# Feed forward by seven block products, hidden units through DRAM, and the third layer norm moved into the attention turns

## Chip, cores and metric

One core of one Trainium2 chip. The metric is the device time of one execution in microseconds (us), the median of repeated runs. PE is the matrix engine, PEld its weight load, DVE the vector engine, ACT the scalar engine, POOL is GpSimd, SP is the queue that issues all DMAs.

## What is computed

One decoder layer on x, 16 sequences of 128 rows by 1024 columns, all in fp32:

```
x = x + attn(layernorm(x))              # qkv 1024 -> 3072, clip, layer norm of q and k, 32 heads, Wout
x = x + xattn(layernorm(x), ctx)        # 8 heads of 64, linear attention, column norm
h = layernorm(x)
a = h @ W1.T ; b = h @ W3.T             # 1024 -> 2752, weights as 4-bit words times a scale per group of 64
x = x + (silu(a) * b) @ W2.T            # 2752 -> 1024
```

## The kernel before

**Arithmetic.** A big product is made in three passes: an operand is split into a high part (ACT copies it into the engine's reduced fp32 type) and a low part (DVE subtracts the high part from it), and PE sums high by high, high by low and low by high. Each matmul here is 128 x 128 weights by 512 columns.

**Phases.** `qkv_phase` writes q, k and v to DRAM. `attention_phase` runs 17 turns, `turns(eng, turn)`: turn b does the self attention of sequence b (`own`), the cross attention of sequence b-1 (`cross`), and prepares sequence b+1 (`ahead`). A turn has 12 steps t, written out in one fixed order for each engine (`turn_tensor`, `turn_scalar`, `turn_vector`, `turn_gpsimd`, `turn_sync`), and ends with the projections. In a step, PE forms scores (L527), turns the normalised scores (L519), forms queries of the cross attention (L537), keys (L558, even steps) and turns the keys (L564, odd steps) in the PSUM pair `pair_k`, which ACT empties (L669 into kT). DVE adds the bias to the scores (L481), takes maxima and sums. The last operation of a sequence is `res<-v_in,res` on POOL (L728, semaphore `fin`), after which SP stores `res` to x2 in DRAM.

**Feed forward.** `feed_forward_phase` handles the 16 sequences in two halves of 8. A half first loads x2 into `acc` (L1003, L1007, L1018), normalises it (`LayerNormT`: statistics on DVE L63 to L69, `normalise` on POOL L76 and L79, eight transposes on PE L86, high part on ACT L92, low part on DVE L96). Then it loops over 22 tiles of 128 hidden units, two to a group. For a tile, DVE unpacks the words (L1077 shifts, L1087 times scale), ACT takes the high part (L1042), DVE the low part (L1091). PE forms a and b for two slices of 512 rows: 4 products of 24 matmuls (L312). ACT forms silu (L1054), DVE multiplies (L1115), ACT and DVE split the result (L1056, L1119). Between tiles PE adds the previous group's part of the w2 product (L1214, 16 outputs of 6 matmuls), which DVE adds into `acc` (L1127). The last tile has 64 units, a and b sharing one product. w1, w3 and w2 are unpacked once per half, so twice.

The loops are hardware loops over pairs of groups, and every engine runs its own list in order, with semaphores between them.

## Time and profile before

| | us |
|---|---|
| median of 3 runs (3300.97 to 3302.31) | 3301.26 |
| span of the profiled execution | 3302.6 |
| qkv phase, about | 0 to 562 |
| attention phase, about | 562 to 1812 |
| feed forward | 1812.1 to 3302.6 |

The profiled execution has no time of its own beside its span; the span is 1.3 us above the median of the runs. The busy share of PE is that of modelled intervals that overlap, so waits are read from the chain of waits and from the timeline.

### The profile page before, as it was taken

To read this page: it belongs to the slowest core of one execution; us is meant where nothing else is said; L and a number is where in the kernel's file an instruction comes from. 1 tells how busy PE (TensorE), PEld (TensorE's weight loads), DVE (VectorE), ACT (ScalarE), POOL (GpSimd) and SP (SyncE) were. 2 spreads that over 40 slices of the span, in tenths; PEclk is the share of its full clock that TensorE was granted. 3 is DMA by queue.
4 is the path that set the end of the run, shared out by engine and by line. 5 is a ranking of instruction groups with operands and counts; after the bars stand their busy time and mean duration, and the time that the engine had idled before them with its cause. 6 is when DMAs were issued, how large, how long until landed. Compare 5 with 4: busy or idle time off the path is not lost. (4 is left out here: it accounts for less than half of the span.)

```text
span 3302.6 us, 41842 instructions
## 1 busy us (share of the span) xinstructions
PE 3132.5 (95%) x15136; PEld 2396.3 (73%) x15136; DVE 1772.9 (54%) x2927; ACT 1045.8 (32%) x2356; POOL 506.7 (15%) x525
## 2 busy tenths in 40 slices
PE   7999998799999999999996799999999899999999
PEld 6888886566666666666663688888887788888887
DVE  5311112466666666666663655555555655555555
ACT  2100000566666566666651211111111211111111
POOL 2100000233333333333332100000000100000000
PEclk9999999899999999999997899999999999999999
DMA  4222223111111111111110422222122521222222
GB/s 143 93 71 74 73 73 109 48 39 38 38 51 48 40 38 39 50 38 51 38 33 25 134 82 54 72 65 80 54 81 73 153 66 54 81 81 54 61 75 78
DMA packets 83350, 218.73 MB, mean 66 GB/s; under 512 B 11984, under 2 KB 18256, under 8 KB 81232
## 3 DMA queue, kind: packets, MB, share of 16 engines
q1 hardware_dynamic: 83280, 217.78, 21.7%
q8 instruction: 46, 0.75, 0.1%
q14 instruction: 24, 0.20, 0.0%
HBM read 175.79 MB, written 41.94 MB: 66 GB/s over the span
## 5 line engine op out<-in xcount | busy, mean ns | idle before, releaser
L1042 ACT ACTIVATE w_hi<-words 128x1024 fp32r<-128x1024 f32 x134 | 142.5, 1064 | 697.5 <-DVE words L1087 697.5
L312 PE MATMUL ff_ps<-h_xT_hi,w_hi 128*128 128x512 f32 x1376 | 344.0, 392 | 13.2 <-DVE h_xT_lo L96 13.2
L1127 DVE TENSOR_TENSOR acc<-ff_po,acc 128x512 f32<-128x512 f32 x352 | 243.0, 692 | 210.0 <-PE ff_po L1214 209.3
L312 PE MATMUL ff_ps<-h_xT_lo,w_hi 128*128 128x512 f32 x1376 | 341.8, 391 | 0.0
L312 PE MATMUL ff_ps<-h_xT_hi,w_lo 128*128 128x512 f32 x1376 | 339.8, 389 | 0.0
L312 PEld LDWEIGHTS ff_ps<-h_xT_hi,w_hi 128*128 128x128 f32 x1376 | 259.8, 189 | 68.4 <-issue 8.8
L312 PEld LDWEIGHTS ff_ps<-h_xT_lo,w_hi 128*128 128x128 f32 x1376 | 260.0, 189 | 54.4
L312 PEld LDWEIGHTS ff_ps<-h_xT_hi,w_lo 128*128 128x128 f32 x1376 | 258.3, 188 | 53.6
L282 DVE TENSOR_SCALAR qkv_out<-qkv_acc 128x512 f32<-128x512 f32 x96 | 66.4, 692 | 396.5 <-PE qkv_acc L312 396.5
L1115 DVE TENSOR_TENSOR gate<-gate,ff_ps 128x512 f32<-128x512 f32 (+1 forms) x88 | 60.3, 686 | 345.4 <-PE ff_ps L312 344.6
L656 ACT ACTIVATE scores<-scores,neg_max 128x128 f32<-128x128 f32 x512 | 199.1, 390 | 122.6 <-DVE neg_max L487 122.6
L1214 PE MATMUL ff_po<-w_hi,h_hi 128*128 128x512 f32 x704 | 219.8, 394 | 8.7 <-ACT h_hi L1056 8.7
L1214 PE MATMUL ff_po<-w_hi,h_lo 128*128 128x512 f32 x704 | 218.5, 392 | 0.0
L1214 PE MATMUL ff_po<-w_lo,h_hi 128*128 128x512 f32 x704 | 218.5, 392 | 0.0
L312 PE MATMUL qkv_acc<-w_hi,xT_hi 128*128 128x512 f32 x768 | 193.0, 394 | 9.5 <-DVE w_lo L255 9.5
L312 PE MATMUL qkv_acc<-w_lo,xT_hi 128*128 128x512 f32 x768 | 190.8, 391 | 0.0
L312 PE MATMUL qkv_acc<-w_hi,xT_lo 128*128 128x512 f32 x768 | 189.8, 389 | 0.0
L231 ACT ACTIVATE w_hi<-w_stage 128x512 fp32r<-128x512 f32 x56 | 35.4, 632 | 452.5 <-DMA w_stage<-in_w_attn 452.5
L697 POOL TENSOR_TENSOR scores<-scores,row_rec 128x512 f32<-128x512 f32 x128 | 133.1, 1040 | 296.1 <-DVE row_rec L765 296.1
L312 PEld LDWEIGHTS qkv_acc<-w_hi,xT_hi 128*128 128x128 f32 x768 | 144.1, 189 | 39.3 <-DVE w_lo L255 9.9
L312 PEld LDWEIGHTS qkv_acc<-w_lo,xT_hi 128*128 128x128 f32 x768 | 145.2, 189 | 30.3
L1087 DVE TENSOR_TENSOR words<-words,sc 128x1024 f32<-128x1024 int32 x134 | 164.2, 1225 | 4.6
(156 smaller groups left out, 5196.5 us busy)
## 6 DMA issues: line engine op xcount, KB each, us to landing
words<-in_w SPq DMA_DIRECT2D x90, 512.0 KB, 3.5
qkv<-qkv_out SPq DMA_DIRECT2D x96, 256.0 KB, 2.0
words<-in_w SPq DMA_DIRECT2D x176, 128.0 KB, 4.0
sc<-in_s SPq DMA_DIRECT2D x88, 256.0 KB, 4.3
qk_in<-qkv SPq DMA_DIRECT2D x16, 1024.0 KB, 5.0
w_stage<-in_w_attn SPq DMA_DIRECT2D x56, 256.0 KB, 2.9
qkv_rows<-in_x SPq DMA_DIRECT2D x16, 512.0 KB, 3.8
ctx_in<-in_context SPq DMA_DIRECT2D x16, 512.0 KB, 3.8
```

Of the source, the lines that this page charges most:

```text
L231: nc.scalar.activation(dst[:, r, :], stage[:, r % 2, :], ACT.Copy).then_inc(w_hi_done, 1)
L282: nc.vector.tensor_scalar(res[:, :], acc[:, t % BANKS, :], CLIP, -CLIP, ALU.min, ALU.max).then_inc(clipped, 1)
L312: last = nc.tensor.matmul(out, left, right, start=n == 0, stop=n == len(pairs) - 1)
L656: last = nc.scalar.activation(sc[:, t % SR, j, :], sc[:, t % SR, j, :], ACT.Exp, bias=neg_max[:, t, j:j + 1], accum_out=row_sum[:, t, j:j ...
L697: nc.gpsimd.tensor_tensor(sc[:, n % SR, :, :], sc[:, n % SR, :, :], row_rec[:, n, :].unsqueeze(2).to_broadcast([P, HG, P]), ALU.mult).then ...
L1042: nc.scalar.activation(dst, src, ACT.Copy).then_inc(s["split_hi"], 1)
L1087: nc.vector.tensor_tensor(dst, src, scale, ALU.mult).then_inc(s["scaled"], 1)
L1115: nc.vector.tensor_tensor(gate[sl][0:units, :], gate[sl][0:units, :], b, ALU.mult).then_inc(s["product"], 1)
L1127: nc.vector.tensor_tensor(cols, po[:, o % 4, :], cols, ALU.add).then_inc(s["added"], 1)
L1214: last = nc.tensor.matmul(po[:, o % 4, :], l[:, at], r[:, par, :], start=n == 0, stop=n == 5)
```

## The change

**Block products.** For each tile of 128 units, W1 and W3 stand as two rows of blocks, and the input dimension in two halves of 512: blocks A11, A12 (w1) and A21, A22 (w3). The normalised input of a half is four blocks, its two halves of the input dimension by two slices of 512 rows. Seven products of 12 matmuls (Winograd's form of Strassen's scheme) take the place of 4 of 24. They need four sums of weight blocks, `sums` (S1 to S4), which POOL forms for every tile (`left_sums`), and four of input blocks, t1 to t4, formed once for a half by DVE (`first_difference`) and POOL (`right_sums`), each of 128 x 2048, and then split by ACT and DVE in `start_half`. Three of the products go onto a PSUM bank that already holds a partial sum, after ACT has copied it out (`snap`); DVE adds the pieces (`combine`, four for a tile). Gate one is multiplied by DVE, gate two by POOL. The last tile of a half is done in the old way, by 24 and 36 matmuls (`merged_tile`).

**Hidden units through DRAM.** The gated units go to a DRAM tensor `hid`. After both halves a w2 stage follows: for 6 chunks of 4 tiles (the last of 2) and 4 groups of 512 rows, the units are loaded (`hraw`, 1 MB), ACT takes the high part, POOL the low part (`hidden_low`, 128 x 2048), and PE forms 8 outputs of 12 matmuls. w2 is unpacked once, in two word buffers `words2`. `acc` of all 16 sequences is loaded from x2 at the start of this stage.

**Layer norm in attention.** For turns 2 to 16 the output of sequence b-2 (in `res`) is normalised, turned and stored to `xt`: statistics on DVE at step 2, normalisation on POOL at step 3, eight transposes on PE in `pair_k` and the copy on ACT at step 4, the store on SP. Sequence 15's follows the last turn.

The loops of the feed forward are written out in straight code.

```diff
-        with ExitStack() as ph:
-            feed_forward_phase(nc, sb, pb, sem, holds, ph, w13, s13, w2, s2, shifts, x2, out, ident, half_neg,
-                               ln_stats, ln_moments)
+        feed_forward_phase(nc, sb, pb, sem, w13, s13, w2, s2, shifts, x2, xt, hid, out)
 
 
...
+    def post_statistics(dve, b):
+        dve.wait_ge(s["fin"], b - 1)
+        nc.vector.bn_stats(x2_st[:, 0:6], res[:, 0:N])
+        nc.vector.bn_stats(x2_st[:, 6:12], res[:, N:D]).then_inc(s["x2_stats"], 1)
+        dve.wait_ge(s["x2_stats"], b - 1)
+        hold_dve()
+        nc.vector.bn_aggr(x2_mo[:, 0:2], x2_st[:, :]).then_inc(s["x2_aggr"], 1)
+        dve.wait_ge(s["x2_aggr"], b - 1)
+        nc.vector.tensor_scalar(x2_mo[:, 2:3], x2_mo[:, 0:1], -1.0, None, ALU.mult)
+        nc.vector.tensor_scalar(x2_mo[:, 3:4], x2_mo[:, 1:2], EPS, None, ALU.add).then_inc(s["x2_mom"], 1)
+
+    def post_normalise(pool, b, projected):
+        pool.wait_ge(s["x2_mom"], b - 1)
+        nc.gpsimd.tensor_tensor(x2_mo[:, 4:5], x2_mo[:, 3:4], neg8[:, 0:1], ALU.pow).then_inc(s["x2_rstd"], 1)
+        pool.wait_ge(s["x_done"], projected)
+        pool.wait_ge(s["x2_rstd"], b - 1)
+        hold_pool()
+        nc.gpsimd.tensor_scalar(x2n[:, :], res[:, :], x2_mo[:, 2:3], x2_mo[:, 4:5], ALU.add, ALU.mult).then_inc(
+            s["x2_norm"], 1)
+
+    def post_turn(pe, b):
+        pe.wait_ge(s["x2_norm"], b - 1)
+        for k in range(KT):
+            last = nc.tensor.transpose(pair_k[:, k * P:(k + 1) * P], ln_columns(x2n[:, :], k), ident[:, :])
+        last.then_inc(s["x2_turned"], 1)
+
+    def post_copy(act, b):
+        act.wait_ge(s["x2_turned"], b - 1)
+        nc.scalar.activation(flat(x2t[:, :, :]), pair_k[:, :], ACT.Copy).then_inc(s["x2_copied"], 1)
+
+    def post_store(sp, b):
+        sp.wait_ge(s["x2_copied"], b - 1)
+        sp.dma_start(xt[b - 2, :, :, :], x2t[:, :, :]).then_inc(s["xt_stored"], 16)
+
...
+            if post and t == 4:
+                if own:
+                    pe.wait_ge(s["kt_out"], b * XT + 2)
+                post_turn(pe, b)
...
+                if post and i == 2:
+                    pe.wait_ge(s["x2_copied"], b - 1)
...
+            if post and t == 4:
+                post_copy(act, b)
...
+            if post and t == 3:
+                post_normalise(pool, b, 2 * b)
...
+            if post and t == 2:
+                post_statistics(dve, b)
...
+            if post:
+                dve.wait_ge(s["xt_stored"], (b - 1) * 16)
...
+        turn(eng, 0, True, False, True, False)
+        turn(eng, 1, True, True, True, False)
+        with eng.Fori(2, NB - 1) as b:
+            turn(eng, b, True, True, True, True)
+        turn(eng, NB - 1, True, True, False, True)
+        turn(eng, NB, False, True, False, True)
...
+            post_turn(pe, NB + 1)
...
+    A11, S1, S2, A12, S3, S4, A22 = range(OPS)
+    R21, R22, R11, R12 = 2, 3, 4, 5
+    b11, b21, b22, t1 = [(plain[2 * i], plain[2 * i + 1]) for i in range(4)]
+    t2, t3, t4 = (zone[0], zone[1]), (zone[3], zone[5]), (zone[2], zone[4])
+    right = [b11, t1, t2, b21, t3, b22, t4]
...
+    def source(u, j):
+        w = [words[u % 2][:, i, :].bitcast(F32) for i in range(2)]
+        if merged(u):
+            return w[0][:, j * N:(j + 1) * N]
+        return {A11: w[0][:, 0:N], A12: w[0][:, N:D], A22: w[1][:, N:D], S1: sums[:, 0, :], S2: sums[:, 1, :],
+                S3: sums[:, 2, :], S4: sums[:, 3, :]}[j]
...
+            def load_right(hf):
+                if hf:
+                    sp.wait_ge(s["ab_done"], base(NT - 1))
+                for at in (R11, R12, R22, R21):
+                    i, sl = {R11: (0, 0), R12: (0, 1), R21: (1, 0), R22: (1, 1)}[at]
+                    t = hf * HALF + sl * SETS
+                    for j in range(SETS):
+                        sp.dma_start(raw[:, at, j * N:(j + 1) * N].rearrange("p (k n) -> p k n", k=HK),
+                                     xt[t + j, :, i * HK:(i + 1) * HK, :]).then_inc(r_in[at - R21], 16)
...
+            def load2(w):
+                if w >= 2:
+                    sp.wait_ge(s["w2_done"], w - 1)
...
+            sp.wait_ge(s["ab_done"], base(TILES - 1))
+            load2(0)
+            load2(1)
+            load_hidden(0)
+            load2(2)
+            load2(3)
+            store(TILES - 1)
+            load_hidden(1)
+            sp.wait_ge(s["ab_done"], base(TILES))
+            for t in range(NB):
+                sp.dma_start(acc[:, t, :], x2[t, :, :]).then_inc(acc_in[t // SETS], 16)
+            for m in range(CHUNKS2 * SETS):
+                if 4 + m < NT:
+                    load2(4 + m)
...
+            def right_sums(hf):
+                pool.wait_ge(s["x_t1"], hf + 1)
+                pool.wait_ge(r_in[R22 - R21], (hf + 1) * 64)
+                nc.gpsimd.tensor_tensor(raw[:, 1, :], raw[:, R22, :], raw[:, 0, :], ALU.subtract).then_inc(s["x_t"], 1)
+                pool.wait_ge(s["x_t"], 3 * hf + 1)
+                pool.wait_ge(r_in[0], (hf + 1) * 64)
+                pool.wait_ge(s["x_lo"], OPS * hf + 1)
+                nc.gpsimd.tensor_tensor(raw[:, R11, :], raw[:, R21, :], raw[:, 1, :], ALU.subtract).then_inc(
+                    s["x_t"], 1)
+                nc.gpsimd.tensor_tensor(raw[:, R12, :], raw[:, R22, :], raw[:, R12, :], ALU.subtract).then_inc(
+                    s["x_t"], 1)
+
...
+            def hidden_low(m):
+                n = inner(m // SETS)
+                pool.wait_ge(s["h_split"], m + 1)
+                nc.gpsimd.tensor_tensor(flat(h_lo[m % 2][:, 0:n, :]), flat(hraw[m % 2][:, 0:n, :]),
+                                        flat(h_hi[m % 2][:, 0:n, :]).bitcast(F32), ALU.subtract).then_inc(
+                    s["h_ready"], 1)
...
+            hidden_high(0)
+            w2_high(0)
+            silu_merged(TILES - 1, 0)
+            w2_high(1)
+            w2_high(2)
+            silu_merged(TILES - 1, 1)
+            w2_high(3)
...
+            def start_half(hf):
+                first = hf * NT
+                first_difference(hf)
+                left_low(first, A11)
+                right_low(hf, 0, b11, R11)
+                right_low(hf, 1, t1, 0)
+                left_low(first, S1)
+                left_low(first, S2)
+                dve.wait_ge(s["x_t"], 3 * hf + 2)
+                right_low(hf, 2, t2, 1)
+                right_low(hf, 3, b21, R21)
+                left_low(first, A12)
+                right_low(hf, 4, b22, R22)
+                for j in (S3, S4, A22):
+                    left_low(first, j)
+                right_low(hf, 5, t3, R12)
+                right_low(hf, 6, t4, R11)
+
             dve.wait_ge(s["shifts"], 16)
...
+            unpack2(0)
+            unpack2(1)
+            gate_merged(TILES - 1, 0)
+            w2_low(0)
+            w2_low(1)
+            unpack2(2)
+            gate_merged(TILES - 1, 1)
+            unpack2(3)
+            w2_low(2)
+            w2_low(3)
+            for m in range(CHUNKS2 * SETS):
+                add(m, 0)
+                if 4 + m < NT:
+                    unpack2(4 + m)
+                add(m, 1)
+                add(m, 2)
+                add(m, 3)
+                add(m, 4)
+                if 4 + m < NT:
+                    w2_low(4 + m)
+                for n in range(5, 2 * SETS):
+                    add(m, n)
 
         @block.tensor
...
+            def whole(u):
+                first = u % NT == 0
+                hf = u // NT
+                k = whole_before(u)
+                a = chain[u % 2]
+                old = u - 1
+                into = (a, bank_c, a, bank_b, a, bank_d, a)
+                ready = (1, 2, 3, 4, 6, 5, 7)
+                for j in range(OPS):
+                    pe.wait_ge(s["w_lo"], base(u) + j + 1)
+                    if first:
+                        pe.wait_ge(s["x_lo"], OPS * hf + ready[j])
+                    if j == A11 and u >= 2:
+                        pe.wait_ge(s["h0_done"], u - 1)
+                    if j == S1 and k:
+                        pe.wait_ge(s["combined"], 4 * k - 1)
+                    if j == A12 and u:
+                        if merged(old):
+                            pe.wait_ge(s["merged_done"], hf)
+                        else:
+                            pe.wait_ge(s["combined"], 4 * k - 2)
+                    if j == S4 and k:
+                        pe.wait_ge(s["combined"], 4 * k)
+                    if j in (S2, S3, A22):
+                        pe.wait_ge(s["snapped"], 3 * k + {S2: 1, S3: 2, A22: 3}[j])
+                    multiply(into[j], terms(u, j, right[j]), j in (S2, S3, A22))
+
+            def merged_tile(u):
+                pe.wait_ge(s["w_lo"], base(u) + 2)
+                pe.wait_ge(s["h0_done"], u - 1)
+                multiply(chain[u % 2], terms(u, 0, b11) + terms(u, 1, b21))
+                pe.wait_ge(s["combined"], 4 * whole_before(u) - 2)
+                multiply(bank_b, terms(u, 0, t1) + terms(u, 0, b11) + terms(u, 1, b22))
+
+            def outputs(m):
...
+            def outputs(m):
+                q = m // SETS
+                n = inner(q)
+                pe.wait_ge(s["h_ready"], m + 1)
+                pe.wait_ge(s["w2_done"], 4 * q + n)
```

## Rows read from the trace of the kernel before

**Rows 1.** The page, busy time of the engines, share of the span, instructions.

```profile
PE 3132.5 (95%) x15136; PEld 2396.3 (73%) x15136; DVE 1772.9 (54%) x2927; ACT 1045.8 (32%) x2356; POOL 506.7 (15%) x525
```

**Rows 2.** Chain of waits in order of time, feed forward: start, us, what.

```profile
2503.08 21.77 PE ff_po L1214 x96
2524.88 0.04 DVE acc L1127
...
2594.63 54.72 PE ff_ps L312 x240
...
3258.66 0.03 DVE acc L1127
...
3273.86 24.92 PE ff_po L1214 x96
```

**Rows 3.** Groups by line and form, whole span: busy, mean ns, idle before.

```profile
L1087 DVE TENSOR_TENSOR words<-words,sc 128x1024 f32<-128x1024 int32 x134 | 164.2, 1225 | 4.6
...
L1077 DVE TENSOR_SCALAR words<-words,shift 128x1024 int32<-128x1024 int32 x90 | 72.7, 807 | 2.5 <-DMA sc<-in_s 2.5
...
L1042 ACT ACTIVATE w_hi<-words 128x1024 fp32r<-128x1024 f32 x134 | 142.5, 1064 | 697.5 <-DVE words L1087 697.5
...
L728 POOL TENSOR_TENSOR res<-v_in,res 128x1024 f32<-128x1024 f32 x16 | 37.5, 2347 | 6.6 <-DVE v_in L821 6.6
```

**Rows 4.** Timeline, DVE and POOL at one time: start, duration, operation.

```profile
36.17 1.20 POOL L79 TENSOR_SCALAR qkv_rows<-qkv_rows,ln_moments 128x1024 f32<-128x1024 f32 x1
36.48 1.42 DVE L255 TENSOR_TENSOR w_lo<-w_stage,w_hi 128x512 fp32r<-128x512 f32 x1
...
1823.64 1.22 DVE L1091 TENSOR_TENSOR w_lo<-words,w_hi 128x1024 fp32r<-128x1024 f32 x1
1823.88 1.74 POOL L76 TENSOR_TENSOR ln_moments<-ln_moments,half_neg 128x1 f32<-128x1 f32 x1 [4.43 <-DVE ln_moments L69]
```

**Rows 5.** Timeline, end of attention and start of the feed forward.

```profile
1806.77 2.34 POOL L728 TENSOR_TENSOR res<-v_in,res 128x1024 f32<-128x1024 f32 x1 [6.63 <-DVE v_in L821]
1812.26 0.82 SPq L1003 DMA_DIRECT2D acc<-x  x2
...
1815.67 0.69 DVE L63 BATCH_NORM_STATS2 ln_stats<-acc 128x6 f32<-128x512 f32 x1 [9.05 <-DMA acc<-x]
...
1817.60 0.56 POOL L76 TENSOR_TENSOR ln_moments<-ln_moments,half_neg 128x1 f32<-128x1 f32 x1 [8.49 <-DVE ln_moments L69]
...
1819.51 1.97 PE L86 MATMUL ff_ps<-ident,h_rows 128*128 128x128 f32 x8 [14.28 <-POOL h_rows L79]
...
1840.71 3.75 PE L312 MATMUL ff_ps<-h_xT_hi,w_hi 128*128 128x512 f32 x8 [3.00 <-DVE h_xT_lo L96]
```

**Rows 6.** Timeline, turn 15 of attention, steps 2 to 4.

```profile
1614.80 0.69 DVE L481 SCALAR_TENSOR_TENSOR scores<-bank_s,alibi 128x512 f32<-128x512 f32 x1
...
1618.79 1.11 ACT L673 ACTIVATE kE<-pair_k,kneg 128x1024 f32<-128x1024 f32 x1 [0.38 <-DVE kneg L758]
...
1620.05 1.10 PE L564 MATMUL pair_k<-ident,kE 128*128 128x128 f32 x8
...
1622.77 0.60 PE L519 MATMUL bank_p<-ident,scores 128*128 128x128 f32 x4
1622.84 1.00 ACT L669 ACTIVATE kT<-pair_k 128x1024 f32<-128x1024 f32 x1
```

**Rows 7.** One line's instructions (the load of q and k, once a turn): count, first and last start.

```profile
L500 SPq DMA_DIRECT2D qk_in<-qkv x15: 328/332/333, 637.4 to 1653.0; - x15
```

**Rows 8.** Windows: length, busy (x) of PE, PEld, DVE, ACT, POOL; granted clock, DMA share, GB/s.

```profile
1620.00:1640.00 20.00, 19.96 (x126) 12.90 (x124) 15.79 (x33) 16.05 (x48) 9.01 (x10) 1.00 0.11 32
```

**Rows 9.** Windows of 3 us at the loads of the feed forward, same columns.

```profile
1818.00:1821.00 3.00, 1.49 (x7) 1.50 (x8) 1.00 (x2) 0.00 (x0) 1.35 (x2) 0.50 1.04 412
```

**Rows 10.** DMA issues of w2: count, KB each, us to landing; one issue in the timeline.

```profile
sc<-in_s SPq DMA_DIRECT2D x88, 256.0 KB, 4.3
...
1830.83 0.60 SPq L998 DMA_DIRECT2D sc<-in_s  x1
```

More of the change, by code:

```diff
@@ L879, in _ @@
             turns(act, turn_scalar)
+            act.wait_ge(s["xt_stored"], (NB - 1) * 16)
+            post_copy(act, NB + 1)
         @block.vector
@@ L992, in load2, with load13 @@
-            def load2(tile, u):
-                sp.wait_ge(split[2], u + 1)
+            def load13(u):
+                if u >= 2:
+                    sp.wait_ge(s["w_lo"], base(u - 1))
+                for mat in range(1 if merged(u) else 2):
+                    sp.dma_start(words[u % 2][:, mat, :], w13[u % NT, mat, :, :]).then_inc(
+                        (w1_in, w3_in)[mat][u % 2], 16)
+                    if mat == 0:
+                        sp.dma_start(sc13[u % 2][:, :, :], s13[u % NT, :, :, :]).then_inc(s13_in[u % 2], 16)
@@ L1037, in _ @@
+            for hf in range(2):
+                left_sums(hf * NT)
+                right_sums(hf)
+                for u in range(hf * NT, hf * NT + WHOLE):
+                    if not merged(u + 1):
+                        left_sums(u + 1)
+                    gate(u)
+            for m in range(CHUNKS2 * SETS):
+                hidden_low(m)
         @block.scalar
         def _(act):
-            def high(mat, dst, count):
-                act.wait_ge(s["scaled"], count)
-                src = words[mat][:, :].bitcast(F32)
-                nc.scalar.activation(dst, src, ACT.Copy).then_inc(s["split_hi"], 1)
@@ L1059, in _, with left_high @@
-            for mat in range(2):
-                high(mat, flat(w13_hi[0][:, mat, :, :]), mat + 1)
-            for hf in range(2):
-                for t in range(HALF):
-                    ln.high(act, hf * HALF + t, t, turn[t])
-                def group(j, parity, first, last):
-                    for e in range(2):
-                        tile(hf * NT + j * 2 + e, e, 2 if e else parity, first, LAST_UNITS if last and e else P)
-                groups(act, group)
+            def left_high(v, j):
+                if merged(v) or j in (A11, A12):
+                    act.wait_ge(scaled[0], v + 1)
+                elif j == A22:
+                    act.wait_ge(scaled[1], whole_before(v) + 1)
+                else:
+                    act.wait_ge(s["summed"], 4 * whole_before(v) + {S1: 1, S2: 2, S3: 3, S4: 4}[j])
+                if room_for(v, j):
+                    act.wait_ge(s["ab_done"], room_for(v, j))
+                nc.scalar.activation(ring_hi[:, slot(v, j), :], source(v, j), ACT.Copy).then_inc(s["w_hi"], 1)
@@ L1236, in _, with terms, multiply @@
-            outputs(2 * GROUPS - 1, (0, 2))
+            def terms(u, j, op):
+                at = slot(u, j)
+                (hi, lo) = op
+                return [(l[:, at, k * P:(k + 1) * P], r[:, :, k, :])
+                        for l, r in ((ring_hi, hi), (ring_hi, lo), (ring_lo, hi)) for k in range(HK)]
+            def multiply(out, pairs, onto=False):
+                for n, (l, r) in enumerate(pairs):
+                    last = nc.tensor.matmul(out.rearrange("p (a b) -> p a b", a=SETS), l, r,
+                                            start=not onto and n == 0, stop=n == len(pairs) - 1,
+                                            skip_group_check=onto)
+                last.then_inc(s["ab_done"], 1)
@@ L1239, in lay_out_ffn @@
+            for u in range(TILES):
+                if merged(u):
+                    merged_tile(u)
+                else:
+                    whole(u)
+            for m in range(CHUNKS2 * SETS):
+                outputs(m)
+    keep.close()
 def lay_out_ffn(w1, s1, w2, s2, w3, s3):
```

619 lines of the change are left out of this document (369 added, 250 removed).

## Prediction

> **What bounds the kernel now.** I read the page first: PE is busy 95% of the span [rows 1]. That number says little, so I went to the chain of waits. In the feed forward it runs through PE almost without a break, at one pace: 96 matmuls of 512 columns in 21.77 us, 0.2267 each [rows 2]. The reader is to see that pace, and how little of the feed forward is anything else. Its matmuls are 4128 for w1/w3 (2 halves of 21 tiles of 96 and one of 48) and 2112 for w2 (22 groups of 96), together 6240 x 0.2267 = 1414.5 us. The phase lasts 1812.1 to 3302.6, 1490.5 us, so 76 are lost, in three places. At the start: by 2524.9, 2976 matmuls are done (674.6 us), so the start costs 2524.9 - 1812.1 - 674.6 = 38.2. Between the halves: from 2524.9 to 2594.6, 69.7 us pass for 192 matmuls (43.5), so 26.2. At the end: from 3258.7, 43.9 us for 144 matmuls (32.6), so 11.3, of which 3.8 follow the last matmul [rows 2].
>
> The attention phase is another case. A turn takes (1653.0 - 637.4)/14 = 72.5 us [rows 7]. In its steps PE is busy 19.96 of 20 us, DVE 15.8, ACT 16.1, POOL 9.0 [rows 8]. Three engines are nearly full, in fixed orders, so work put there is not free.
>
> **Matmuls.** A whole tile has 7 x 12 = 84 matmuls for 96, a last one 24 + 36 = 60 for 48. That is 2 x (21 x 84 + 60) = 3648, and w2 has 6 x 4 x 8 outputs with 3 x 22 in all, 2112 as before. So 480 fewer: -108.8 us at the pace of [rows 2]; the shapes are the same, so I keep the pace.
>
> Does PE keep it inside a tile, now 19.0 us long? DVE has two unpacks of 0.8 + 1.2, seven low parts and five adds or gates of 0.6 to 0.7: 12 us. ACT has 12 copies of 0.6, POOL 5 operations of half of 2.35: 6 us [rows 3]. The only tight link is the copy before a product adds onto a bank: ACT needs 0.6 (half of its 1.06 [rows 3]), and another product of 2.7 us stands in between each time. I take no loss; what it costs otherwise is a rival.
>
> **The start of a half.** Let F be when DVE begins the first difference of 2048 elements. Sizes: DVE 2 x 1.15 = 2.3, ACT 2.0, POOL 2 x 2.35 = 4.7, less what is fixed in each, 4.5 [rows 3]. Do DVE and POOL run side by side? The rows say no: a POOL operation that takes 0.56 alone [rows 5] took 1.74 beside a DVE subtraction of two SBUF tensors, and a DVE low part of 0.7 took 1.42 while POOL held on for its 1.20 [rows 4]. Each waits for the other to end. In `start_half` nearly every DVE operation reads two SBUF tensors. So POOL gets in only where DVE stops: DVE does the difference, b11, t1 and three low parts to F+8.5, POOL then two operations to F+17.6, DVE t2, b21, b22 and low parts to about F+27, POOL the third, and t3 is split by F+33 to F+35. The first tile's products 1 and 2 run early, 3 and 4 at F+20 to 28, and 5 to 7 from about F+34. PE is then cold (after a pause, eight matmuls took 3.75 us [rows 5]), so the tile ends at F+45, 26 us later than with 84 matmuls begun at F at full pace. The lost time is F+26. Were POOL not held off, t3 would be split at F+23 and the loss F+14: 12 us less at each half.
>
> The Trainium skill (GPSIMD Engine Reference, section 8, Key points) says that GpSimd shares its SBUF interfaces with VectorE and contends with instructions that have two SBUF inputs. The trace agrees, and shows that the wait is for a whole instruction; the rule has no size, so by it alone the loss lies anywhere from F+14 to F+26.
>
> First half: the loads land at 412 GB/s [rows 9], 3.2 MB up to the second block, about 3 us after the issue: F = 10.8 after the phase starts, and POOL still owes two weight sums (2.1). Lost 10.8 + 26 + 2.1 = 38.9 for 38.2: +0.7. Second half: merged products end 13.6 us after the last whole tile, silu and gate bring F to 15.5. Lost 15.5 + 26 - 13.6 = 27.9 for 26.2: +1.7. The removed layer norms therefore give back nothing by themselves.
>
> **Into the w2 stage.** Let E be the end of tile 42. PE has 13.6 us left to do. SP issues two stores, then six DMAs each for w2 tiles 0 and 1, 0.6 each [rows 10], and only at E+9.2 the first hidden block, landed at E+14.2. ACT has that copy first in its list, so silu of the last tile, whose product was ready at E+5.4, waits to E+17; behind it the gate, low part 0 (after POOL's 4.5 us: E+22). `words2` has two buffers, so the load of w2 tile 2 waits for low part 0, and takes 3.8 + 4.3 us [rows 10]: E+29.4; tile 3 follows at E+33.2. Unpack, high, gate, unpack, high, low of 1 to 2 us each: the fourth low part is there at E+39.1, and only then may the first output start. PE stands 25.5 us, plus 2.5 of cold start: 28. I looked whether 8 MB for `acc`, queued ahead of w2 tile 4, stop the adds: at 412 GB/s they have landed by E+63, where PE needs the second add at E+66; just hidden. At the end 3.8 remain. 28 + 3.8 - 11.3 = +20.5. From below, the old gap of 7.5 would do (-20); from above, some 45 if the `acc` loads run at half that rate (+17).
>
> **The layer norm in attention.** One turn, on [rows 6]. DVE at step 2: from 1815.67 to 1817.60 the same five operations took 1.9 us [rows 5]; L481 moves from 1614.8 to 1616.6. Behind it wait the key maximum, ACT's exponential (1618.79) and PE's turn of keys 1 (1620.05): to 1621.8. POOL's part (1.9 [rows 5]) falls where POOL waits. At step 4 PE waits first for kT of keys 1 to leave `pair_k`: that copy, at 1622.84 for 1.0, now ends at 1625.7, while PE would be there at 1624.5. Then 8 transposes, 0.9 (the eight of L564 take 1.1 with the last one's way). L519 comes at 1626.6 for 1622.77: 3.8 us late. ACT's copy of 1.0 delays probT, but keys 2 come later still. PE is full from there on, so nothing is won back. 14 turns: 53.2. Bounds: the transposes alone, 1.1 (15 in all, -38), or the chain wholly exposed, 1.9 + 1.9 + 1.1 + 1.0 = 5.9 (83, +29). The rows of PE full and DVE at 15.8 of 20 put it between. Turn 16 is slow and cold: 1.9 + 2.0 = 3.9. After the last turn `res` is ready at 1809.1 [rows 5]; statistics 1.9, POOL 1.9, transposes 2.0, copy 1.0 come ahead of the store: +7.0 with waits. Attention +64.1.
>
> **Sum.** 3302.6 - 108.8 + 0.7 + 1.7 + 20.5 + 64.1 = 3280.8; the span is 1.3 above the median of the runs, so 3280. I call a change within 0.2% (6.6 us) none: that is about what a measurement can tell.
>
> **Rivals.**
> Light turns (15%): the wait at step 4 and the DVE delay vanish in slack; a turn costs 1.5. For it: DVE still has 4 us in 20 free. Against: PE has none [rows 8]. 3280 - 14 x 2.3 = 3248.
> Engines side by side (11%): POOL not held off, 24 less: 3256. Against: [rows 4].
> Exposed turns, slower (11%): the whole post chain of 5.9 us lies on the turn, because ACT's copy in front of probT stalls PE's next products too. 3280 + 14 x 2.1 = 3309. It decides from a turn cost of 5.8 on, where the sum passes 3307.9 (slower by 0.2%). For it: ACT 16.1 of 20 us.
> The seven products don't deliver (12%): ACT's order makes PE wait for a copy in each tile. From 1 us a tile, 42 in all: 3322 and more; at 2.6 us the saving is gone. For it: ACT waits in order for sums, products and adds; against: the slack worked out above.
> Mine (51%): 3280, own range 3263 to 3300, with a quarter of it above 3294.7.
>
> **Numbers.** Faster: 0.38 of mine, 0.15 and 0.11, some 0.01 of the rest: 0.65. Same: 0.12 of mine and 0.03 of the exposed turns: 0.15. Slower: 0.20. The range leaves out the far ends of light turns with others and of stalls above 1 us: 3238 to 3320.
>
> **What would show it.** Span from the end of qkv to the feed forward longer by 64, a turn of 76.3 by the first starts of the load of q and k. PE idle for kT at step 4. In a whole tile, 84 matmuls in 19.0 us with no idle. Before product 3 of a half PE waits for DVE, DVE for POOL, and POOL's 2048 operations are drawn out beside DVE. One idle stretch of about 25 us between the merged tile 43 and the first output, at whose end stands the fourth low part. I am wrong if turns grow by under 2 or over 5 us, or if tiles show waits of PE for ACT.

## The result: 10.7 us faster, where 21 were forecast

| | median of the runs | range | span of the profiled execution |
|---|---|---|---|
| before (6 runs beside it) | 3302.47 us | 3300.97 to 3303.78 | 3302.6 |
| after (6 runs) | 3291.82 us | 3287.89 to 3293.58 | 3289.7 |

The ratio is 0.9966, with a 95% interval of 0.9956 to 0.9976: 0.34% faster, and surely more than 0.2%. The forecast was 3280, a gain of 0.64%. So the sign was right and half of the gain is missing. The tables below go by the spans of the two profiled executions, which differ by 12.9 us where the medians differ by 10.7: the span before is 1.3 us above its median, the one after 2.1 below. The first line of the page, for [rows 1]:

```profile
PE 3027.4 (92%) x14656; PEld 2308.0 (70%) x14656; DVE 1808.2 (55%) x2933; ACT 1178.8 (36%) x2618; POOL 940.9 (29%) x781
```

PE is less busy by some 100 us and its share falls from 95% to 92%: the matmuls are gone, and idle time has come. Where it is, the chain of waits says, for [rows 2]. Columns: start, length, what.

```profile
1864.73 6.75 DMA raw<-xt
1871.57 2.94 DVE raw L1400
...
1907.57 410.84 PE ff_room L1536 x1800
2318.46 0.61 issue
...
2320.37 2.21 DVE raw L1400
2322.66 9.34 POOL raw L1208
2332.07 4.92 POOL raw L1212
2336.99 13.93 POOL raw L1214
2350.94 1.92 ACT xz L1254
2352.88 2.30 DVE xz L1406
2355.28 396.96 PE ff_room L1536 x1740
...
2761.79 7.40 DMA hraw<-hid
...
2807.29 18.31 DMA sc<-in_s
...
2828.55 457.36 PE ff_room L314 x2004
3285.93 0.69 DVE acc L1445
```

Read it with the arithmetic of the forecast. The feed forward starts at 1859.1 (1812.2 before). The first half has 1824 matmuls, 413.5 us, and ends at 2318.4: 45.8 lost. The second has 1764 up to the end of tile 42 at 2752.3, 399.9 us: 34.0 lost. Then 2172 matmuls, 492.4 us, up to 3289.7: 45.1 lost, 3.8 of it behind the last matmul.

| term | forecast | measured |
|---|---|---|
| 480 matmuls fewer | -108.8 | -108.8 (the pace is the same) |
| attention | +64.1 | 1859.1 - 1812.2 = +46.9 |
| start of the first half | +0.7 | 45.8 - 38.2 = +7.6 |
| start of the second half | +1.7 | 34.0 - 26.2 = +7.8 |
| into the w2 stage and end | +20.5 | 45.1 - 11.3 = +33.8 |
| sum | -21.8 | -12.7 (the spans: -12.9) |

The pace holds inside the tiles. In the busy time by window PE works 20.00 of 20 us, VectorE 13.3, ScalarE 7.5, GpSimd 7.6 (in this order, behind the weight loads; then the granted clock):

```profile
2400.00:2420.00 20.00, 20.00 (x90) 16.53 (x90) 13.32 (x17) 7.51 (x14) 7.56 (x6) 1.00 0.28 86
```

**A turn of attention** is longer by 3.0 us, not 3.8: from the 1st to the 14th addition onto `res` (turns 2 to 14) the mean distance was 72.94 and is 75.92. Before, 8 of these 13 turns take 72.35 and 5 take 73.88; after, all lie between 75.83 and 76.05. In steps 2 to 4 of one turn, for [rows 6], PE, then VectorE and ScalarE in the timeline (a bracket is the idle time ahead of the instruction and who ended it):

```profile
1657.03 1.09 PE L617 MATMUL pair_k<-ident,kE 128*128 128x128 f32 x8 [0.89 <-ACT kE L728]
1657.96 1.95 PE L628 MATMUL pair_o<-kT,qk_in 128*128 128x128 f32 x16
1660.87 1.16 PE L524 MATMUL pair_k<-ident,x2n 128*128 128x128 f32 x8 [0.96 <-ACT kT L724]
...
1650.18 0.69 DVE L503 BATCH_NORM_STATS2 x_st<-res 128x6 f32<-128x512 f32 x1
...
1662.07 1.02 ACT L529 ACTIVATE x2t<-pair_k 128x1024 f32<-128x1024 f32 x1 [1.25 <-PE pair_k L524]
```

The wait for kT at step 4 is there (0.96), and so is the one that VectorE's statistics cause by way of the key's exponential (0.89).

The two kinds of turn before the change differ by PE's clock. In 4 us of two neighbouring turns at the same place (busy time by window, columns as above), shortly behind a wait of 2.11 us that every turn has, the granted clock was 0.57 and 1.00 (mostly 1.2 GHz, and 2.4 GHz):

```profile
1467.00:1471.00 4.00, 4.00 (x12) 1.95 (x11) 1.55 (x3) 2.79 (x11) 1.04 (x1) 0.57 0.70 248
1541.00:1545.00 4.00, 4.00 (x15) 1.79 (x13) 2.66 (x5) 3.69 (x15) 1.04 (x1) 1.00 0.65 241
```

Such a stretch makes a turn of the kernel before 1.5 us longer. In the changed kernel 6 of the 13 turns have one (0.57 in 1496 to 1500), and they are only 0.2 longer, because in them PE's waits for VectorE are gone but for 0.11: its own work ahead of them takes longer. PE, turn of keys 1 in such a turn, without a bracket:

```profile
1505.33 1.09 PE L617 MATMUL pair_k<-ident,kE 128*128 128x128 f32 x8
```

**The start of a half.** GpSimd, ScalarE, VectorE and PE of the second half, timeline, with F = 2320.3, for [rows 4, 5]:

```profile
2322.66 9.33 POOL L1208 TENSOR_TENSOR raw<-raw 128x2048 f32<-128x2048 f32 x1 [7.81 <-DVE raw L1400]
2332.07 4.92 POOL L1212 TENSOR_TENSOR raw<-raw 128x2048 f32<-128x2048 f32 x1
2336.96 13.95 POOL L1214 TENSOR_TENSOR raw<-raw 128x2048 f32<-128x2048 f32 x1
...
2350.94 3.71 ACT L1254 ACTIVATE xz<-raw 128x2048 fp32r<-128x2048 f32 x2 [11.32 <-POOL raw L1214]
2354.56 0.58 ACT L1261 ACTIVATE ends<-ff_room 128x512 f32<-128x512 f32 x1
...
2327.51 10.03 DVE L1394 TENSOR_TENSOR ring_lo<-sums,ring_hi 128x512 fp32r<-128x512 f32 x2
...
2355.28 3.75 PE L1536 MATMUL ff_room<-xz,ring_hi 128*128 128x512 f32 x8 [18.08 <-DVE xz L1406]
```

A sum by GpSimd takes 4.9 where VectorE is held off or done, 9.33 and 13.95 beside it, and two low parts of VectorE (0.68 each alone) take 10.03 beside GpSimd. The matmul group at 2355.28, F+35.0, is product 3. The forecast had products 3 and 4 at F+20 to 28 and product 5 at F+34. So five products, not three, come after F+35, and the next tile's first starts at 2371.26, F+51.0 for F+45. The bracket blames VectorE's low part of `xz`; but product 3 needs `t2`, whose low part ended at 2339.7. Line L1261, which ends 0.14 us ahead of product 3, looks innocent, and is the cause (first experiment).

**Into w2.** The queue of SP, ScalarE, PE and one line of VectorE, timeline; tile 42 ends at E = 2752.3:

```profile
2761.79 0.52 SPq L1148 DMA_DIRECT2D hraw<-hid  x1
...
2769.21 1.91 ACT L1322 ACTIVATE h_hi<-hraw 128x2048 fp32r<-128x2048 f32 x1 [18.32 <-DMA hraw<-hid]
2771.97 0.57 ACT L1273 ACTIVATE ends<-ff_room 64x512 f32<-64x512 f32 x1
...
2794.47 2.05 PE L314 MATMUL ff_room<-w_hi,h_hi 128*128 128x512 f32 x4 [28.65 <-DVE w_lo L1437]
...
2825.63 1.00 DVE L1367 TENSOR_SCALAR words<-words,shift 128x512 int32<-128x512 int32 x2 [23.29 <-DMA sc<-in_s]
...
2828.55 2.07 PE L314 MATMUL ff_room<-w_hi,h_hi 128*128 128x512 f32 x4 [6.50 <-DVE acc L1445]
```

The chain is as forecast, link by link: block issued at E+9.5 for E+9.2, silu behind it, fourth low part, first output at E+42.2 for E+39.1 (the block took 7.4 us to land, not 5). What the forecast called just hidden is not: the adds stop for w2 tile 4, whose last piece took 18.31 us to land behind the `acc` loads, PE stands 6.5 us more and starts cold (at 1.2 GHz, 8 matmuls in 3.6 us for 1.8) once more.

### The profile page after: what moved, and what is told of

It is laid out like the page before. It is cut to its first block and busy times, and to the rows that moved or that the text cites. A ratio compares the mean times of both kernels' runs of the same rounds, so it can differ in the third digit from the quotient of the medians.

```text
span 3289.7 us, 40227 instructions
## 1 busy us (share of the span) xinstructions
PE 3027.4 (92%) x14656; PEld 2308.0 (70%) x14656; DVE 1808.2 (55%) x2933; ACT 1178.8 (36%) x2618; POOL 940.9 (29%) x781
## 5 line engine op out<-in xcount | busy, mean ns | idle before, releaser
L1536 PE MATMUL ff_room<-xy,ring_hi 128*128 128x512 f32 x1424 | 358.8, 395 | 40.4 <-DVE xy L1406 25.0
L1536 PEld LDWEIGHTS ff_room<-xy,ring_hi 128*128 128x128 f32 x1424 | 271.3, 191 | 99.1 <-issue 32.9
L1536 PE MATMUL ff_room<-xz,ring_hi 128*128 128x512 f32 x1008 | 252.5, 393 | 29.4 <-DVE xz L1406 29.4
L1536 PEld LDWEIGHTS ff_room<-xz,ring_hi 128*128 128x128 f32 x1008 | 191.2, 190 | 70.1 <-issue 30.3
L314 PE MATMUL ff_room<-w_hi,h_hi 128*128 128x512 f32 x704 | 193.4, 393 | 35.2 <-DVE w_lo L1437 28.7
L1261 ACT ACTIVATE ends<-ff_room 128x512 f32<-128x512 f32 x126 | 75.3, 598 | 388.4 <-PE ff_room L1536 388.4
L314 PE MATMUL ff_room<-w_lo,h_hi 128*128 128x512 f32 x704 | 192.5, 392 | 0.0
L314 PE MATMUL ff_room<-w_hi,h_lo 128*128 128x512 f32 x704 | 192.5, 392 | 0.0
L1536 PE MATMUL ff_room<-xy,ring_lo 128*128 128x512 f32 x712 | 192.1, 392 | 0.0
L314 PEld LDWEIGHTS ff_room<-w_hi,h_hi 128*128 128x128 f32 x704 | 133.9, 191 | 63.8 <-issue 29.0
L1367 DVE TENSOR_SCALAR words<-words,shift 128x1024 int32<-128x1024 int32 (+1 forms) x130 | 143.0, 1113 | 58.5 <-DMA sc<-in_s 43.3
```

The source lines that it names most:

```text
L314: last = nc.tensor.matmul(out, left, right, start=n == 0, stop=n == len(pairs) - 1)
L1261: nc.scalar.activation(ends[u % 2][:, n, :], chain[u % 2], ACT.Copy).then_inc(s["snapped"], 1)
L1367: last = nc.vector.tensor_scalar(w[:, at], w[:, at], shift[:, 2 * kind:2 * kind + 1], shift[:, 2 * kind + 1:2 * kind + 2], ALU.logical_shi ...
L1536: last = nc.tensor.matmul(out.rearrange("p (a b) -> p a b", a=SETS), l, r, start=not onto and n == 0, stop=n == len(pairs) - 1, skip_group ...
```

## Experiments

Each kernel is the changed kernel with the edit that is named or shown. Times are medians; the interval is that of the ratio to the kernel before, and "against after" is the difference to 3291.8. Three stretches of each profiled execution tell where a difference lies: P1 from the first load of the feed forward to the second half's first product, P2 from there to the first output of w2, P3 to the end of the span. The changed kernel has 466.4, 469.0 and 495.2.

**ScalarE's copies of the first tile ahead in its queue.** In ScalarE's `start_half`:

```diff
                 for j in (A12, S3, S4, A22):
                     left_high(first, j)
+                snap(first, 0)
+                snap(first, 1)
                 act.wait_ge(s["x_t"], 3 * hf + 3)
...
                 right_high(hf, t4[0], R11)
+                snap(first, 2)
```

For the first tile of a half the three are taken out of their old places in the list of the tile.

> ScalarE's three copies of the first tile's end bank are put into the list of a half's start: two ahead of the wait for the last two right blocks, the third behind them. My theory: after the second product of a half PE does not wait for a low part of a right block, as the releaser column says, but for the first of these copies, which stands in ScalarE's list behind the copies of the last two blocks (in the changed kernel PE starts product 3 at 2355.28, 0.2 us after that copy of 0.58 at 2354.56). Then products 3 and 4 run at once when their blocks are there, some 13 us earlier, product 5 starts when the last block but one is split, where product 3 starts now, and the first tile ends two products, 5.4 us, earlier; if the sums of the next tile are just in time, 5.4 in each half: 3291.8 - 10.9 = 3281. If the next tile's sums (GpSimd at 2361.48 to 2367.9) are late for it, 2 to 4 a half: 3284 to 3288. Rival, the releaser column is right and PE waits for VectorE's low parts of right blocks: product 3 starts where it does now, and nothing is gained, 3291 to 3293.

3282.6 us, -9.2 against after; ratio 0.9938 (0.9924 to 0.9951). P1 461.5 (-4.9), P2 464.9 (-4.1), P3 as it was. Timeline of ScalarE and PE, second half, F = 2319.2:

```profile
2338.41 0.57 ACT L1261 ACTIVATE ends<-ff_room 128x512 f32<-128x512 f32 x1
...
2339.13 3.75 PE L1543 MATMUL ff_room<-xz,ring_hi 128*128 128x512 f32 x8 [4.65 <-ACT ends L1261]
...
2354.20 3.51 PE L1543 MATMUL ff_room<-xz,ring_hi 128*128 128x512 f32 x8 [7.22 <-issue]
...
2368.08 2.09 PE L1543 MATMUL ff_room<-xy,ring_hi 128*128 128x512 f32 x8 [1.31 <-DVE ends L1417]
```

Product 3 runs at F+20, as my forecast had it, and the bracket now names the copy. The rival, that the releaser column is right, is out. At 2368.08 PE waits 1.31 more for an add of VectorE (L1417), so a half gains 4 to 5 us, a little less than the 5.4 expected; GpSimd's sums, which the expectation feared, are not what it waits for.

**Only the first of these copies.** `snap(first, 0)` alone is moved.

> Of the three early copies of the first run only the first is moved ahead of the wait for the last two right blocks. Theory: products 3 and 4 then run early as there, but product 5 adds onto the bank that the second copy reads, and that copy still stands behind the first high part of the next tile, which waits for VectorE's unpack behind the whole list of the half's start (2359.39 in the changed kernel, the copy at 2360.56). So product 5 starts at about F+41, where it starts now, and nothing is gained: 3290 to 3293. Rival, the first copy is the only link: product 5 starts with the split of its block and 4 to 5 us a half are gained, 3282 to 3285.

3291.5 us, -0.3; 0.9967 (0.9955 to 0.9979). P1 466.1, P2 468.0. ScalarE and PE:

```profile
2361.00 0.63 ACT L1251 ACTIVATE ring_hi<-words 128x512 fp32r<-128x512 f32 x1 [4.75 <-DVE words L1391]
2361.54 0.58 ACT L1261 ACTIVATE ends<-ff_room 128x512 f32<-128x512 f32 x1
...
2362.26 3.61 PE L1538 MATMUL ff_room<-xz,ring_hi 128*128 128x512 f32 x8 [13.18 <-ACT ends L1261]
```

Products 3 and 4 ran early (2341.83), and PE then stood 13.18 us for the second copy, which is behind the next tile's first high part. One link taken out moved the wait to the next and gained nothing; with the second and third it was worth 9 us.

**VectorE makes the right sums.** First GpSimd's list, then VectorE's; `right_sum` makes one of the three.

```diff
                 left_sums(hf * NT)
-                right_sums(hf)
...
                 right_low(hf, 1, t1, 0)
+                right_sum(hf, 0)
                 left_low(first, S1)
                 left_low(first, S2)
+                right_sum(hf, 1)
+                right_sum(hf, 2)
```

> GpSimd's three sums of right blocks of 2048 elements are made by VectorE, between its low parts. Theory of mutual exclusion (each of the two engines holds off the other for a whole instruction when VectorE reads two SBUF tensors): VectorE gets 3 x 2.2 = 6.6 us more work, but loses the 10 us in which two low parts of 0.6 each are drawn out, and the 12 us in which it ends and waits for GpSimd's last sum. In the second half: F (first difference) to the split of the last block 28.4 us of back to back work, the last copies by F+26, product 3 at F+27 for F+35 now, so -8 a half: 3276, with 3272 to 3282 as the range. Rival, no exclusion: GpSimd's sums were hidden and VectorE's list is just 6.6 us longer, then product 3 comes at F+35 or later and the time is 3290 to 3305.

3278.2 us, -13.7; 0.9926 (0.9913 to 0.9940). P1 460.2 (-6.2), P2 461.6 (-7.4). VectorE and PE, F = 2316.0:

```profile
2323.18 2.28 DVE L1399 TENSOR_TENSOR raw<-raw 128x2048 f32<-128x2048 f32 x1
2325.38 1.28 DVE L1381 TENSOR_TENSOR ring_lo<-sums,ring_hi 128x512 fp32r<-128x512 f32 x2
...
2342.71 3.75 PE L1538 MATMUL ff_room<-xz,ring_hi 128*128 128x512 f32 x8 [13.58 <-DVE xz L1405]
```

The same two low parts take 1.28 for 10.03, and product 3 starts at F+26.7, as expected (F+27). 6.8 us more work (three sums of 2.28) on the busier engine make the half shorter by 6 to 7. That is the exclusion of [rows 4], and here its price.

**The first hidden block ahead of the w2 loads.** `load_hidden(0)` is issued before the last store of a whole tile.

> The load of the first block of hidden units is issued ahead of the store of tile 42's units and of the twelve loads of w2 tiles 0 and 1, everything else as it is. Now it is issued at 2761.79 and lands at 2769.19, and ScalarE, GpSimd and the load of w2 tile 2 stand behind it. Theory of the chain (hidden block, ScalarE's copy, silu, gate, low part 0, load of w2 tile 2, unpack, gate, low part 3, first output): ScalarE then waits only for w2 tile 0, unpacked at 2763.9; silu at 2765, low part 0 done by 2771 for 2776, and the first output at 2789 for 2794.5: -5.5 us, 3286. Rival, the loads of w2 tiles (0.6 us of issue each, landing 4 to 5 us later) set the end and not this block: the gap stays at 28.7 and the time at 3291 to 3293.

3284.8 us, -7.0; 0.9943 (0.9929 to 0.9956). P1 467.0 and P3 494.2 (+0.6 and -1.0), P2 462.7 (-6.3); PE waits 22.53 for the first output, not 28.65.

**The same, and each low part directly behind its tile.**

```diff
+            gate_merged(TILES - 1, 0)
             unpack2(0)
-            unpack2(1)
-            gate_merged(TILES - 1, 0)
             w2_low(0)
+            gate_merged(TILES - 1, 1)
+            unpack2(1)
             w2_low(1)
             unpack2(2)
-            gate_merged(TILES - 1, 1)
+            w2_low(2)
             unpack2(3)
-            w2_low(2)
             w2_low(3)
```

This is VectorE's list; on ScalarE silu of the last tile goes ahead of w2 tiles 0 and 1 in the same way.

> The early hidden block as in the run before, and the order of the entry into the w2 stage on ScalarE and VectorE: silu and gate of the last tile's first half ahead of w2 tile 0, and each low part directly behind its own tile's high part, ahead of the unpack of the next tile. Theory: the two buffers of words are what the chain hangs on; with the early block low part 0 ended 2772.9, of which 4.4 us are the wait for w2 tile 1 and its unpack. The load of w2 tile 2 is issued 4.5 us earlier, that of tile 3 right behind it, and the first output starts 4.5 us earlier than with the early block alone: 3284.8 - 4.5 = 3280. Rival: with two buffers the loads of tiles 2 and 3 are apart now instead of together and tile 3, the last, lands where it did: 3284 to 3286.

3280.0 us, -11.8; 0.9927 (0.9913 to 0.9940). P2 459.5, 3.2 less than with the early block alone, and P3 491.0: 3.2 less as well, because the stop for w2 tile 4 shrinks from 5.93 to 2.59. The sum is as expected; its place is only partly the first output.

**Residual loads behind the w2 loads.** `load_acc(g)` issues the four loads of group g.

```diff
-            for t in range(NB):
-                sp.dma_start(acc[:, t, :], x2[t, :, :]).then_inc(acc_in[t // SETS], 16)
+            load_acc(0)
             for m in range(CHUNKS2 * SETS):
                 if 4 + m < NT:
                     load2(4 + m)
+                if m < SETS - 1:
+                    load_acc(m + 1)
```

> Of the 16 loads of the residual (8 MB) only the first group of four stands ahead of the load of w2 tile 4; each other group is issued behind the load of the w2 tile of one group earlier. Theory: the 6.5 us in which PE waits at 2828.55 for an add come from w2 tile 4, whose last piece took 18.3 us from issue to landing behind the residual; with it comes a cold start of 2.8 us (12 matmuls in 5.9 for 3.2). Both go: -9, 3282.5. Rival, it is the volume and not the order: the same bytes must land in the same stretch, and the stop comes one or two groups later: 3289 to 3294.

3282.1 us, -9.8; 0.9938 (0.9925 to 0.9952). P3 485.0 (-10.2); from the first output PE has no idle time in the entry any more. It was the order, not the volume.

**The layer norm left out of the turns.**

> In turns 2 to 16 the whole layer norm of x2 is left out (VectorE's statistics, GpSimd's normalise, PE's eight transposes and their wait for kT, ScalarE's copy); the store of xt stays, but stores a constant, and only the one behind the last turn is made in full. Theory: the extra 46.9 us of the attention phase are this work in the turns (14 turns of 3.0, which is less than the 3.8 of my step) and the 7.4 behind the last turn, so turns go back to about 72.5 and the time to 3291.8 - 41 = 3251, of which turn 16 gives back nothing. Rival, part of the longer turn is the store of xt and its place at the head of the queue of loads: then turns stay above 73.5 and the time above 3262.

3248.9 us, -43.0; 0.9838 (0.9825 to 0.9852). A turn takes 72.97, as before the change; the feed forward starts at 1817.8, 5.6 later than before: the part behind the last turn is 7.4 longer, and `res` is ready for it 1.8 earlier. So the store of xt costs the turns nothing.

**Only transposes, wait and copy left out.**

> In turns 2 to 16 only PE's eight transposes, their wait for kT and ScalarE's copy are left out; VectorE's statistics and GpSimd's normalise stay, and the store of xt stores a constant. My step had 1.9 us of VectorE ahead of the key maximum and another 1.9 for the wait, the transposes and the copy, one behind the other. Theory of the chain: both count, so the turn falls by about 1.9 of its 3.0: 3265, with 3262 to 3272. Rival one, PE is full and all of it is PE's: the turn falls by 2.9 to 3.0, 3250 to 3254, and the statistics cost nothing. Rival two, VectorE's delay is all of it and the transposes lie in time in which PE would wait anyway: 3285 to 3292.

3262.8 us, -29.0; 0.9878 (0.9862 to 0.9893). A turn takes 73.80. Both parts count: statistics and normalise 73.80 - 72.97 = 0.83, transposes, wait and copy 75.92 - 73.80 = 2.12. The 0.83 is a mean of two kinds: in turns at full clock the statistics cost 73.71 - 72.41 = 1.30 (PE's waits of 0.37 and 0.89), in turns with a stretch at 1.2 GHz next to nothing (73.90 and 73.86). (The profiled execution is the slowest of the four, and its turn 16 took 59.9; see the end.)

**The layer norm two steps later.**

> The same layer norm two steps later in the turn: statistics at step 4 of VectorE, where it waits 2.5 us for PE (idle before the start at 1663.37), normalise at step 5, the transposes at step 6 ahead of the product with probT, the copy behind ScalarE's exponentials, and product 3 of the keys waits for it. Theory: what costs is not the work but what stands behind it in step 2 to 4 (key maximum, exponential, keys 1), so the statistics go into a wait and PE's transposes cover the copy: 1 to 2 us less a turn, 3264 to 3278. Rival, PE is full in every step, so transposes and what they hold up cost the same anywhere: 3288 to 3293, or more if step 6 is the fuller one.

3312.0 us, +20.1; 1.0029 (1.0018 to 1.0039): slower than even the kernel before. Neither theory. A turn takes 77.30. PE at step 6:

```profile
1690.75 1.05 PE L524 MATMUL pair_k<-ident,x2n 128*128 128x128 f32 x8
1691.73 0.42 PE L599 MATMUL pair_o<-probT,v_in 128*32 128x128 f32 x8
1694.76 1.95 PE L611 MATMUL pair_k<-ctx_in,wqk_sb 128*128 128x512 f32 x4 [2.60 <-ACT x2t L529]
```

ScalarE is in its exponentials up to 1693.6, the copy comes behind them, and PE waits 2.60 for `pair_k`, and 0.45 for keys at step 5: more than the 0.96 + 0.89 + 0.37 that it saved. That is part of the loss. The clock is the other: turns at full clock take 76.29 (75.84 in the changed kernel), but 8 of the 13 turns, for 6, have a stretch at 1.2 GHz, half of them at this very wait, and take 77.92 (76.02 there), since no wait for VectorE is left to take it up. What matters first is when the bank that the transposes borrow comes free.

**Transposes inside step 4, behind the score product.** On PE the lines go from the head of the step to behind the score product; on ScalarE `post_copy` goes from the head of the step to behind the copy of probT.

```diff
         for t in range(STEPS):
-            if post and t == 4:
-                if own:
-                    pe.wait_ge(s["kt_out"], b * XT + 2)
-                post_turn(pe, b)
...
                 nc.tensor.matmul(bank_s[:, :], qkT[:, 0, t, :], flat(kD[:, t, :, :]), start=True,
                                  stop=True).then_inc(s["s_done"], 1)
+            if post and t == 4:
+                if own:
+                    pe.wait_ge(s["kt_out"], b * XT + 2)
+                post_turn(pe, b)
```

> In step 4 of a turn PE's eight transposes of x2 stand behind the transposes of the scores and the score product instead of ahead of them, and ScalarE's copy of them behind that of probT. Nothing is left out. Theory: of the 2.1 us a turn that the transposes and the copy cost (3.0 less the 0.85 that stay without them), 0.96 is PE's wait for the copy of kT before the first transpose; 1.5 us of other matmuls now stand there, and only the transposes themselves and the tail of the copy stay: -0.9 a turn, 14 turns, 3279, with 3275 to 3284. Rival: the run with the layer norm in step 6 lost 1.4 us a turn because PE waited 2.6 us for ScalarE's copy; here too the copy is later, and product 2 of the keys waits for it: 3288 to 3300.

3276.4 us, -15.4; 0.9921 (0.9907 to 0.9934). A turn takes 74.69, 1.23 less, at the good end of the range. PE, same turn:

```profile
1644.25 1.02 PE L574 MATMUL bank_s<-kD,qkT 128*128 128x512 f32 x2
1645.11 1.05 PE L524 MATMUL pair_k<-ident,x2n 128*128 128x128 f32 x8
1645.99 1.02 PE L588 MATMUL bank_q<-wqk_sb,xn 128*128 128x512 f32 x2
```

No bracket is left on L524, and the transposes cost their own time only.

**Everything together.** First a kernel with the three early copies, VectorE's sums, the early block, the late residual and the later layer norm:

> The edits of the runs with the early snapshots (-9.2), VectorE's sums (-13.7), the early hidden block (-7.0), the late residual loads (-9.8) and the later layer norm (0 to -28) in one kernel. If the four places are separate, as the sum of my steps has them, the first four add up to -39.7: 3252 without the fifth, 3224 to 3252 with it. The first two share the first tile of a half: with VectorE's sums the last right block is split 8 us earlier, and the next tile's sums by GpSimd, which come after two unpacks, may then be what PE waits for; that takes up to 3 us a half back: 3258 at most.

3273.7 us, -18.1; 0.9915 (0.9901 to 0.9928). With the +20.1 of the later layer norm taken off, the other four bring -38.2 of the -39.7 that they bring one by one. P1 455.9, P2 451.6, P3 484.5. Then with the layer norm in step 4 and the order of the entry:

> Early snapshots, VectorE's sums, early hidden block, late residual loads (together 3273.7 with the later layer norm, which alone cost 20: so some 3253), with the order of step 4 (-13 if it works as the theory of its run says) and the order of the entry (-4.5). If the places are separate: 3236, with 3232 to 3241. Rival: what the order of the entry brings is taken back by the residual loads, which then are issued earlier beside w2 tiles 3 and 4: 3240 to 3245.

3236.1 us, -55.8; ratio to the kernel before 0.9800 (0.9787 to 0.9813). P1 456.6, P2 447.3, P3 484.3. The edits bring -59.9 one by one (-9.2, -13.7, -11.8, -9.8, -15.4), so the places are nearly separate, and this kernel is 2.0% faster than the one before.

## Why the prediction missed half of the gain

**Matmuls: right.** The pace is kept, no product in a whole tile waits; the rival of seven products that don't deliver is out.

**Attention: mis-sized by 17 us, in my favour.** I added 1.9 us for VectorE's delay and 1.9 for the wait and the transposes, with the copy at nothing, and said that nothing is won back. The second is 2.12 in the runs. The first is 0.83, and there "PE is full from there on, so nothing is won back" failed: in a turn at full clock VectorE's 1.7 us at step 2 come out at PE as 0.37 + 0.89, and in a turn with a stretch at 1.2 GHz as nothing. My rows were those of a turn at full clock, and there the term was nearly right, 75.84 - 72.35 = 3.5 for 3.8. The forecast did not see that 5 of 13 turns before were of the other kind, where the change costs 76.02 - 73.88 = 2.1. Fourteen turns cost 40.7 for 53.2 (thirteen at 2.99, turn 15 at 1.9). Turn 16 was to cost 3.9 and was 1.5 shorter. The chain behind the last turn was priced at 7.0 and took 7.4.

**Starts of the halves: the step "the first tile's products 1 and 2 run early, 3 and 4 at F+20 to 28" failed.** I had found which operation each product's data come from, and left out one wait in the code: a product that adds onto a bank waits for ScalarE's copy of it, and for the first tile that copy is queued behind the copies of all right blocks. So two more products, 5.4 us, stand behind F+35: the next tile starts at F+51.0 for F+45. The early copies put product 3 at F+20 and gave back 4 to 5 us a half. The first half is the same (5.2 us of its 6.9); the other 1.7 are a later landing (F at 12.5 for 10.8). The mutual exclusion was sized right: the last block but one is split at F+34.9 for F+33 to 35, and with the sums on VectorE product 3 starts at F+26.7. The Trainium skill (SBUF — State Buffer, section "SBUF: two separate sides") states what I had read from [rows 4], that of the two engines the one that starts first keeps the other out for the whole instruction. The trace agrees on the exclusion and shows it reach beyond one instruction: the GpSimd sum of 13.95 us, 4.9 alone, starts in the record at 2336.96 and ends at 2350.91, 4.4 us behind the last of seven VectorE operations in a row (2346.56), so it was kept out for all seven.

**Into w2: +33.8 for +20.5.** 3.1 of the difference are the first output (the hidden block landed after 7.4 us, not 5, behind twelve loads). The other 9 to 10 are the step "just hidden": I let 8 MB land at the full rate, which they did (15 of the 16 loads by E+63.4, the last at E+68.9), and did not ask when w2 tile 4, issued behind them, would land. Its six DMAs landed from E+64.9 to E+73.4, 18.31 us after the issue for the last, and VectorE's next adds stand behind its unpack in program order. The late residual gave back 10.2 there, so the size is shown.

Together: attention 17.2 better than its term, the two starts 6.9 and 6.1 worse, the entry 13.3 worse, 9.1 net: -21.8 becomes -12.7. The rest of the miss is the step from span to median: I took 1.3 us off the span as before, and after the change the median lies 2.1 above it.

So the right sign was luck in part. With attention at the cost that I gave it, and the other terms as measured, the change would have made the kernel some 4.5 us slower. Of my own signs of being wrong (a turn longer by under 2 or over 5 us, waits for ScalarE in the tiles) none came: they did not look at the first tile of a half or at w2 tile 4, where the steps failed.

What stays open: what sets the length of turn 16, and in which turns PE's clock falls.

## What to carry to other kernels

For each instruction on the path write down every semaphore in the code that it waits for, with the place of each setter in its engine's list; a releaser in a profile is only the setter that came last by record, and a setter queued behind another engine's work looks innocent. Work put into a full schedule costs what it holds up: here 1 us of transposes cost 2.1 us at the head of a step, 0.9 in its middle and 3.5 two steps later, by when the borrowed bank came free (the 3.5 with the statistics moved too; in turns at full clock it was 2.6). Look at several turns before you take one as the model: here two kinds of turn, by PE's clock, answered the same work with 3.5 and 2.1 us. Two engines that exclude each other are one engine: 6.8 us of work moved to the busier one shortened the stage; and a bulk load belongs behind the small load that is needed first, even where the bytes fit.

## What the runs showed of the hardware

The granted clock in a thinly used stretch took either level. Busy time by window of 35 us early in turn 16, columns as above, the granted clock third from the right. The kernel before:

```profile
1750.00:1785.00 35.00, 23.31 (x49) 10.31 (x48) 19.93 (x39) 9.14 (x16) 14.04 (x15) 0.56 0.04 15
```

The changed kernel:

```profile
1790.00:1825.00 35.00, 19.14 (x61) 8.73 (x60) 21.70 (x46) 10.06 (x17) 15.98 (x18) 0.84 0.08 31
```

The one without the layer norm in its turns:

```profile
1749.00:1784.00 35.00, 18.58 (x52) 7.67 (x51) 19.53 (x39) 9.14 (x16) 14.06 (x15) 0.80 0.09 31
```

The one without transposes and copy:

```profile
1761.00:1796.00 35.00, 21.74 (x42) 8.88 (x40) 21.27 (x44) 7.76 (x14) 14.90 (x17) 0.55 0.09 31
```

The turn takes 53.7, 52.2, 52.6 and 59.9 us. Most of the stretch is at 2.4 GHz in the second and third. In the first and fourth the mean of 0.56 and 0.55 is nearly all 1.2 GHz. I had first put the short turn of the changed kernel down to the added transposes; the kernel without the layer norm is as fast, so that is not it. Nor need it be the kernel at all: six of the experiments have the attention code of the changed kernel, and their turn 16 took 52.1, 52.5, 53.7, 53.8, 55.1 and 55.1 us, at a mean granted clock of 0.78 to 0.81. Each kernel has one profiled execution, so a difference of some 3 us in this turn is no property of a kernel. What decides the level here is open.

The issue of a DMA itself can be held. On SP's queue in the changed kernel it takes 0.3 to 0.6 us, at times 1.1, but behind the residual loads:

```profile
2808.56 5.02 SPq L1132 DMA_DIRECT2D words<-in_w  x1
```

The semaphore that this load waits for had been set at 2794. With the residual in groups, single issues behind a group still took up to 3.39 us. So what stands behind a bulk load may be late in its issue as well as in its landing.
